# Cross-attention and FFN in one core: the prologue in another order, the first weights over two queues, one scores stage ahead of the second FFN layer

## The chip, the core and the metric

The kernel runs on one core of one Trainium2 chip. Its engines are TensorE (PE in the profile, PEld for its weight loads), VectorE (DVE), ScalarE (ACT) and GpSimd (POOL); SyncE (SP) issues most of the DMAs and ACT the rest. The metric is device time in microseconds (us), the median of the runs shown. Everything is float32 at the edges.

## What is computed

```python
x = x + attention(layernorm(x), ctx)      # 2 x 1024 x 256, context 2 x 77 x 192, 8 heads of 64
x = x + 0.5 * ffn(layernorm2(x))          # inside ffn: residual = its input, h = LN(x) * gamma + beta
# attention: q = x Wq, k = ctx Wk, v = ctx Wv, softmax(q k^T / 8) v, then Wo, + bo
# ffn(x) = x + 0.5 * (silu(h w1 + b1) w2 + b2), w = (q - 128) * scale, scale shared by 128 rows
# w1 is 256 x 1024, w2 is 1024 x 256, both stored as int32 with float scales
```

The second line stands for `x + _ffn_ref(_layernorm(x))`: the FFN's input is a layer norm of x, and the FFN norms it once more.

## The kernel before, in words

**Tiles.** The 2048 rows of x are 16 tiles of 128 rows, handled as eight pairs; pair a has the tiles 2a and 2a+1 (`a` runs from 0 to LAST = 7), pairs 0 to 3 belong to batch 0 and 4 to 7 to batch 1. Nothing is held in a lower precision: each operand of the large products is split in a rounded part (`_hi`) and the rest (`_lo`), both of type float32r, and three products (hi hi, hi lo, lo hi) are summed.

**Prologue, once.** The context is transposed (`ctxT`), keys and values are projected (`project`, L735), Wq is transposed and centred (`transpose_wq`). Then Wq and K of a batch are multiplied to one matrix M (`make_m(b, c)`, L766; halves c = 0, 1, in four parts M b.0 to M b.3), and V and Wo to VW (`make_vw(b, n)`, L779; five blocks in three parts VW b.0 to VW b.2). So the scores of a pair are its transposed rows times M, and its attention output is the transposed probabilities times VW. The int32 weights w1 become float in four pieces, each by ACT (`shift_w1`, then `split_w1`) and POOL (`dequantize_w1`, `lower_w1`), w2 in two halves by DVE (`dequantize_w2`, `lower_w2`) and ACT (L490 to L493).

**A pair.** `x_transposes` (XT), `scores` (S, two tiles of 24 products), softmax on DVE, ACT and POOL (`shift_scores`, `exponential`, `invert_sums`, `normalize`), `prob_transposes` (PT, 5 products), `attention_out` (AO, 15 products), `add_attention` on DVE, the root of the variance on POOL (`rsqrt2`), `make_hn` on DVE, `h_transposes` (HT), `scale_h` on ACT, `split_h` on DVE, `fc1` (four parts of 12 products), `hidden` on ACT (Silu, then the rounded part), `lower_y` on POOL, `fc2` (two tiles of 24 products), `finish_tile` on DVE, and the store.

**What sets the order.** Every engine's program is a list written by hand: TensorE's from L856 on, DVE's from L638, ACT's from L445, POOL's from L323, the DMA queue of SP from L223 and that of ACT from L353. An engine works through its list in that order and waits on semaphores. The accumulators are six names, S0, S1, H0, H1, T0 and T1; the table `order` (L62) says which result goes to which of them and in which turn, and a product waits until the last holder of its accumulator has been read (`emptied`, `wait_freed`). In the steady state a round of TensorE is: scores of pair a, the second FFN layer of pair a-2's second tile, `h_transposes(a-1)`, the first FFN layer of pair a-1 with the transposes of the probabilities of pair a between its parts, attention output of pair a, `x_transposes(a+1)`, and the second FFN layer of pair a-1's first tile.

**Warm-up.** Before the context is there TensorE multiplies zeros (`warm(8)`, L857), and once more while ctxT is copied (L865). A float32 product is two records of PE in the trace, a float32r product one.

**Waits that matter below.** `fc1(0, 0)` stands behind a wait for all four pieces of w1 (L905). `prob_transposes(a, j)` waits for `normalize(a, j)` on POOL. `h_transposes(a)` waits for both tiles of `make_hn(a)`, which wait for POOL's `rsqrt2(a)`. `fc2(0, 0)` waits for the lower parts of w2 (L848), which DVE makes, and for `lower_y`. ACT's `residual(a)` is needed by `add_b2(a)` on POOL, and that by `finish_tile`.

Of the kernel before, what the change touches and what calls it, by code (L numbers as in the profile page):

```python
# [25 lines left out]
def build_program(nc, x, ctx_in, wq, wk, wv, wo, bo, gamma, beta, q1, s1, b1, q2, s2, b2, out):  # L26
# [53 lines left out]
    with ExitStack() as stack:  # L80
# [138 lines left out]
        with nc.Block() as block:  # L219

            @block.sync
            def _(sp):
# [35 lines left out]
            def _(pool):  # L258
# [23 lines left out]
                def rsqrt2(a):  # L282

                    o = a % 2
                    for j in range(UT):
                        pool.wait_ge(mv2_done, a * UT + j + 1)
                        nc.gpsimd.tensor_scalar(vars2[:, o, 1, j:j + 1], mv2[:, o, j, 1:2], 1.0 + EPS, EPS * EPS,
                                                ALU.mult, ALU.add).then_inc(vars2_done, 1)
                        pool.wait_ge(vars2_done, a * 3 + j + 1)
                        nc.gpsimd.tensor_tensor(rstd2[:, o, 1, j:j + 1], vars2[:, o, 1, j:j + 1], neg_half[:, 0:1],  # L290
                                                ALU.pow).then_inc(rstd2_done, 1)
# [686 lines left out]
```

## Time and profile before

| | us |
|---|---|
| median of 3 runs | 189.31 (188.37 to 191.15) |
| the profiled execution | 188.6 |
| its span in the trace | 186.8 |
| PE busy | 180.7 (97%) |
| DVE, ACT, POOL busy | 122.4, 122.5, 116.2 |

The span is the time from the first to the last instruction of the trace; the profiled execution lasted 1.8 us longer than its span. TensorE is busy 97% of the span, but this busy time counts a record from its start to its modelled end, and the records overlap: one lasts about 0.28 us and the next starts 0.11 us after it. So the places where TensorE does nothing are read from the starts of neighbouring records and from the waits, not from the share. The eight rounds look alike from about 58.6 us on; what comes before is the prologue with the pairs 0 and 1.

### The profile page before, as it was taken

The numbers are of one execution on the slowest core, as the hardware profiler recorded it, in microseconds if no ns is written. First come the engines' busy times: TensorE is split into PE (matmuls) and PEld (weight loads), VectorE is DVE, ScalarE is ACT, GpSimd is POOL, SyncE is SP. The second block draws the span as 40 slices with busy tenths as digits, with TensorE's granted clock in tenths as the row PEclk, the third lists the DMA queues.
The fourth block names the chain that finished last, engine by engine and source line by source line (L and its number), as shares of the span: only waits on it lengthen the run. The fifth ranks groups of instructions, "written<-read, shape, count | busy, mean of one in ns | idle before, by whom it ended". The sixth has DMA issues, their size and how long they took to land.

```text
span 186.8 us, 3886 instructions
## 1 busy us (share of the span) xinstructions
PE 180.7 (97%) x1502; PEld 177.0 (95%) x1502; DVE 122.4 (66%) x261; ACT 122.5 (66%) x230; POOL 116.2 (62%) x159
## 2 busy tenths in 40 slices
PE   7999899899899999999999999999999999999994
PEld 7999699689899999999999999999999999999994
DVE  0287988899969464964496557937594768255341
ACT  3287880599918981898368944896289817962580
POOL 5032998569983977099707972597439762776220
PEclk9999999999999999999999999999999999999999
DMA  6997990000000100010001000100001000100101
GB/s 171 325 399 185 357 353 13 2 0 4 2 0 0 60 0 0 4 56 0 4 0 56 4 0 0 33 30 0 0 4 56 0 4 0 56 4 0 56 4 56
DMA packets 9480, 10.72 MB, mean 57 GB/s; under 512 B 2268, under 2 KB 8183, under 8 KB 9335
## 3 DMA queue, kind: packets, MB, share of 16 engines
q1 hardware_dynamic: 8837, 9.70, 15.7%
q10 hardware_dynamic: 626, 0.79, 1.5%
q8 instruction: 12, 0.20, 0.4%
q14 instruction: 5, 0.04, 0.1%
HBM read 8.38 MB, written 2.10 MB: 56 GB/s over the span
## 4 chain that ended last, share of the span: by engine, by line
PE 78%; DVE 9%; POOL 9%; ACT 1%; issue 1%
PE T L852 22%; PE H L838 21%; PE T L823 11%; PE S L802 11%; PE S L809 4%; PE S L755 3%; POOL q_sb L316 3%; POOL w_lo L321 3%; PE S L733 2%; DVE w_lo L631 2%; POOL probs L279 1%; DVE q_sb L625 1%; PE T L740 1%; PE H L740 1%; POOL rstd L290 1%
## 5 line engine op out<-in xcount | busy, mean ns | idle before, releaser
L311 POOL TENSOR_TENSOR y_lo<-y,y_hi 128x512 fp32r<-128x512 f32 x28 | 37.6, 1363 | 2.1 <-ACT y_hi L434 1.6
L279 POOL TENSOR_TENSOR probs<-probs,rsum 128x616 f32<-128x616 f32 x16 | 19.1, 1218 | 31.4 <-DVE rsum L583 31.4
L852 PE MATMUL T<-w_hi,y_hi 128*128 128x256 f32 x128 | 36.7, 286 | 0.6 <-DVE x_sb L594 0.6
L838 PE MATMUL H<-hT_hi,w_hi 128*128 128x256 f32 x128 | 36.7, 287 | 0.1
L838 PE MATMUL H<-hT_lo,w_hi 128*128 128x256 f32 x128 | 35.5, 277 | 0.0
L838 PE MATMUL H<-hT_hi,w_lo 128*128 128x256 f32 x128 | 35.5, 277 | 0.0
L852 PE MATMUL T<-w_lo,y_hi 128*128 128x256 f32 x128 | 35.5, 277 | 0.0
L852 PE MATMUL T<-w_hi,y_lo 128*128 128x256 f32 x128 | 35.4, 277 | 0.0
L430 ACT ACTIVATE y<-H,vec 128x256 f32<-128x256 f32 x64 | 26.5, 467 | 6.6 <-PE H L838 6.6
L403 ACT ACTIVATE probs<-probs,rstd 128x616 f32<-128x616 f32 x16 | 12.9, 807 | 27.1 <-DVE probs L571 27.1
L588 DVE TENSOR_TENSOR pT_lo<-S,pT_hi 128x640 fp32r<-128x640 f32 x16 | 13.1, 823 | 18.1 <-ACT pT_hi L407 18.1
L852 PEld LDWEIGHTS T<-w_hi,y_hi 128*128 128x128 f32 x128 | 24.1, 188 | 0.9 <-DVE x_sb L594 0.9
L838 PEld LDWEIGHTS H<-hT_hi,w_hi 128*128 128x128 f32 x128 | 24.1, 188 | 0.5 <-issue 0.5
L852 PEld LDWEIGHTS T<-w_lo,y_hi 128*128 128x128 f32 x128 | 24.1, 189 | 0.0
L838 PEld LDWEIGHTS H<-hT_lo,w_hi 128*128 128x128 f32 x128 | 24.1, 188 | 0.0
L852 PEld LDWEIGHTS T<-w_hi,y_lo 128*128 128x128 f32 x128 | 24.1, 188 | 0.0
L838 PEld LDWEIGHTS H<-hT_hi,w_lo 128*128 128x128 f32 x128 | 24.1, 188 | 0.0
L823 PE MATMUL T<-vw_hi,pT_hi 128*128 128x256 f32 x80 | 22.4, 280 | 0.0
L823 PE MATMUL T<-vw_lo,pT_hi 128*128 128x256 f32 x80 | 22.1, 277 | 0.0
L823 PE MATMUL T<-vw_hi,pT_lo 128*128 128x256 f32 x80 | 22.1, 277 | 0.0
L434 ACT ACTIVATE y_hi<-y 128x512 fp32r<-128x512 f32 x32 | 20.2, 632 | 1.0
L564 DVE TENSOR_REDUCE smax<-S 128x8 f32<-128x616 f32 x16 | 12.8, 799 | 12.0 <-PE S L802 11.5
(127 smaller groups left out, 460.6 us busy)
## 6 DMA issues: line engine op xcount, KB each, us to landing
q_sb<-in_L_ffn_fc_q SPq DMA_DIRECT2D x2, 1024.0 KB, 8.0
out_x<-x_sb SPq DMA_DIRECT2D x16, 128.0 KB, 1.8
x_sb<-in_x SPq DMA_DIRECT2D x7, 256.0 KB, 8.2
s_sb<-in_L_ffn_fc_scales SPq DMA_DIRECT2D x2, 512.0 KB, 12.0
s_sb<-in_L_ffn_fc_scales SPq DMA_DIRECT2D x1, 1024.0 KB, 7.7
wq_sb<-in_L_xattn_Wq SPq DMA_DIRECT2D x1, 512.0 KB, 5.6
wo_sb<-in_L_xattn_Wo SPq DMA_DIRECT2D x1, 512.0 KB, 8.1
wk_sb<-in_L_xattn_Wk ACTq DMA_DIRECT2D x1, 384.0 KB, 4.1
```

The lines of the kernel that those rows point to most:

```text
L279: nc.gpsimd.tensor_tensor(p, p, rsum[:, j, :].unsqueeze(2).to_broadcast([P, HEADS, J]), ALU.mult).then_inc(norm_done, 1)
L311: nc.gpsimd.tensor_tensor(y_lo[:, two, :], y[:, two, :], f32(y_hi[:, two, :]), ALU.subtract).then_inc(y_lo_done, 1)
L403: nc.scalar.activation(probs[:, j, 0:HJ], probs[:, j, 0:HJ], ACT.Exp, scale=rstd1[:, t:t + 1]).then_inc(exp_done, 1)
L430: ins = nc.scalar.activation(y[:, m, :], r[:, q * W:(q + 1) * W], ACT.Silu, bias=b1_sb[:, m:m + 1])
L434: nc.scalar.activation(y_hi[:, two, :], y[:, two, :], ACT.Copy).then_inc(y_hi_done, 1)
L564: nc.vector.tensor_reduce(smax[:, j, :].rearrange("p (n h) -> p n h", n=2), s, AX_X, ALU.max).then_inc(max_done, 1)
L588: nc.vector.tensor_tensor(flat(pT_lo[:, j, :, :]), ps[bank][:, 0:JC * P], flat(f32(pT_hi[:, j, :, :])), ALU.subtract).then_inc(freed[bank], 1)
L802: ins = mm(o, xt[:, c, j * P:(j + 1) * P], m[:, b, c, h, 0:HALF], start=n == 0, stop=n == len(steps) - 1)
L809: ins = nc.tensor.transpose(r[:, m * P:(m + 1) * P], probs[:, j, m * P:(m + 1) * P], ident[:, :])
L823: ins = mm(r[:, 0:D], p[:, j, m, :], v[:, b * JC + m, :], start=n == 0, stop=n == len(steps) - 1)
L838: ins = mm(r[:, q * W:(q + 1) * W], wt[:, c, m * P:(m + 1) * P], ht[:, c, :], start=c == q == i == 0, stop=c == q == 1 and i == 2)
L852: ins = mm(o, yt[:, m, j * P:(j + 1) * P], wt[:, m, :], start=m == 0 and i == 0, stop=m == M - 1 and i == 2)
```

## The change

The program does the same products, copies and transfers; only three of the warm-up products go, and wk comes by two DMAs where it was one. What moves:

- **Loads.** The first half of wk stays the first DMA of ACT's queue; its second half is the second of SP's, ahead of wq. `warm(8)` is `warm(5)`. `project("K", ...)` waits for both halves.
- **M and VW of batch 1.** `make_m(1, 1)` moves from between the transposes of the probabilities of pair 0 to behind `make_vw(1, 2)`, just ahead of `fc1(0, 0)`, and its two parts share accumulator S0. `make_vw(1, 0)` is cut in two, and its pieces stand around `prob_transposes(0, 0)`.
- **w1.** Its four pieces are now cut so that pieces 0 and 1 are the left columns of both row halves. POOL dequantizes two, normalizes pair 0, lowers two, dequantizes two, makes the roots of pair 0 (`root2`), and only then lowers the last two; `residual_roots` is what was left of `rsqrt2`. `fc1(0, 0)` waits for two pieces, `fc1(0, 2)` for four.
- **Pair 1.** `fc1(0, 2)` stands between the two transposes of probabilities, as in all later pairs. `x_transposes(2)` goes ahead of `attention_out(1, *)`, and `fc2(0, 0)` goes behind `scores(2, *)`, so that the scores of pair 2 (the third) are made first.
- **The other engines** follow: DVE does `stats1(1)` early, takes `lower_w2(1)` behind `add_attention(1, *)`; POOL cuts `lower_y(0, *)` in pieces between the roots of pair 1; ACT does `x_hi(2)` before `hidden(0, 2)` and `residual(0)` behind `exponential(2, 0)`.

In TensorE's list, around the transposes of the probabilities of pair 0 (L809; L786 is VW, L774 is M, L755 a transpose of x or hn), it stood so before:

```order
L755 MATMUL S<-ident,x_sb 128x128 x4
...
L774 MATMUL T<-kT,wqT 128x77
L809 MATMUL S<-ident,probs 128x128 x5
L774 MATMUL H<-kT,wqT 128x77
...
L809 MATMUL S<-ident,probs 128x128 x5
L786 MATMUL H<-wo_sb,vT 128x256 x3
L823 MATMUL T<-vw_hi,pT_hi 128x256
```

And so it stands there now (L838 are the transposes, L814 is VW, L852 the attention output):

```order
L800 MATMUL T<-kT,wqT 128x77
L814 MATMUL H<-wo_sb,vT 128x256
L838 MATMUL S<-ident,probs 128x128 x5
L814 MATMUL H<-wo_sb,vT 128x256 x2
L838 MATMUL S<-ident,probs 128x128 x5
L852 MATMUL T<-vw_hi,pT_hi 128x256
```

One of the three products of VW1.0 now fills the place before the first transposes, two stand between them, and M1's second half is gone from there.

In POOL's list, from the first dequantization of w1 to the first normalization of pair 1, before (L316 dequantizes w1, L279 normalizes, L321 lowers w1, L287 and L290 are the root of the second norm, L272 and L274 that of the first):

```order
L316 TENSOR_TENSOR q_sb<-q_sb,s_sb 128x512 x3
L279 TENSOR_TENSOR probs<-probs,rsum 128x616 x2
L316 TENSOR_TENSOR q_sb<-q_sb,s_sb 128x512
L321 TENSOR_TENSOR w_lo<-q_sb,w_hi 128x512 x4
L272 TENSOR_SCALAR veps<-mv 128x2
L274 TENSOR_TENSOR rstd<-veps,neg_half 128x2
L287 TENSOR_SCALAR vars<-mv 128x1
L290 TENSOR_TENSOR rstd<-vars,neg_half 128x1
```

Now (L319 dequantizes, L280 normalizes, L324 lowers w1, L273 and L275 are the first norm's root):

```order
L319 TENSOR_TENSOR q_sb<-q_sb,s_sb 128x512 x2
L280 TENSOR_TENSOR probs<-probs,rsum 128x616 x2
L324 TENSOR_TENSOR w_lo<-q_sb,w_hi 128x512 x2
L319 TENSOR_TENSOR q_sb<-q_sb,s_sb 128x512 x2
L287 TENSOR_SCALAR vars<-mv 128x1
L290 TENSOR_TENSOR rstd<-vars,neg_half 128x1
L287 TENSOR_SCALAR vars<-mv 128x1
L290 TENSOR_TENSOR rstd<-vars,neg_half 128x1
L273 TENSOR_SCALAR veps<-mv 128x2
L275 TENSOR_TENSOR rstd<-veps,neg_half 128x2
L324 TENSOR_TENSOR w_lo<-q_sb,w_hi 128x512 x2
```

Two of the four lowered pieces of w1 stand behind the roots now, and the roots of the second norm stand ahead of that of the first.

In DVE's list, from the dequantization of w2 to the first maximum of pair 2, now (L650 dequantizes w2, L613 is the lower part of the transposed probabilities, L578 that of VW, L584 that of the transposed x, L656 that of w2, L619 to L623 add the attention output and take its statistics, L629 is hn, L589 the maximum):

```order
L650 SCALAR_TENSOR_TENSOR q_sb<-q_sb,s_sb 128x1024 x2
L613 TENSOR_TENSOR pT_lo<-S,pT_hi 128x640
L578 TENSOR_TENSOR vw_lo<-T,vw_hi 128x512
...
L613 TENSOR_TENSOR pT_lo<-S,pT_hi 128x640
L578 TENSOR_TENSOR vw_lo<-T,vw_hi 128x256
L584 TENSOR_TENSOR xT_lo<-S,xT_hi 128x512
L656 TENSOR_TENSOR w_lo<-q_sb,w_hi 128x1024
L619 TENSOR_TENSOR x_sb<-T,x_sb 128x256
...
L656 TENSOR_TENSOR w_lo<-q_sb,w_hi 128x1024
L629 SCALAR_TENSOR_TENSOR hn<-x_sb,mv,rstd 128x256 x2
L589 TENSOR_REDUCE smax<-S 128x8
```

Before, both halves of w2 were lowered one behind the other ahead of the additions, and the lower part of x stood behind them.

The diff, without the parts that only rename a column or pass an index on:

```diff
              ("M0.0", "H1"), ("M0.1", "T0"), ("M0.23", "S0"), ("VW0.2", "T1"), ("VW0.0", "H0"), ("S0.0", "S0"), ("S0.1", "S1"),
-             ("VW0.1", "T1"), ("XT1", "S1"), ("M1.0", "H1"), ("M1.1", "T0"), ("PT0.0", "S0"), ("M1.2", "H0"), ("M1.3", "T1"), ("PT0.1", "S1"),
-             ("VW1.0", "H1"), ("AO0.0", "T0"), ("AO0.1", "T1"), ("S1.0", "S0"), ("S1.1", "S1"), ("HT0", "H0"), ("VW1.1", "T0"), ("VW1.2", "T1")]
+             ("VW0.1", "T1"), ("XT1", "S1"), ("M1.0", "H1"), ("M1.1", "T0"), ("VW1.0", "H0"), ("PT0.0", "S0"), ("PT0.1", "S1"),
+             ("AO0.0", "T1"), ("AO0.1", "T0"), ("S1.0", "S0"), ("S1.1", "S1"), ("HT0", "H0"), ("VW1.1", "T0"), ("VW1.2", "T1"), ("M1.23", "S0")]
     for a in range(1, NA):
         if a > 1:
-            order += [(f"S{a}.0", "S0"), (f"S{a}.1", "S1"), (f"F2.{a - 2}.1", "T1"), (f"HT{a - 1}", "S0")]
+            order += [(f"S{a}.0", "S0"), (f"S{a}.1", "S1")] + [("F2.0.0", "T0")] * (a == 2) + [(f"F2.{a - 2}.1", "T1"), (f"HT{a - 1}", "S0")]
         order += [(f"F1.{a - 1}.{p}", f"H{1 - p % 2}") for p in range(HP)]
         order += [(f"PT{a}.0", "S1"), (f"PT{a}.1", "S0"), (f"AO{a}.0", "T0"), (f"AO{a}.1", "T1")]
-        order += [(f"XT{a + 1}", "S1")] * (a < LAST) + [(f"F2.{a - 1}.0", "T0")]
+        order += [(f"XT{a + 1}", "S1")] * (a < LAST) + [(f"F2.{a - 1}.0", "T0")] * (a > 1)
...
                 sp.dma_start(ctx_sb[:, :, :], ctx_v).then_inc(ctx_in_sem, 16)
+                sp.dma_start(wk_sb[:, 1, :], wk[CC:DC, :]).then_inc(wk_in, 16)
                 sp.dma_start(wq_sb[:, :, :], wq.rearrange("(n p) f -> p n f", p=P)).then_inc(wq_in, 16)
...
+                def root2(a, j):
                     o = a % 2
...
+                def residual_roots(a):
+                    o = a % 2
                     nc.gpsimd.tensor_scalar(vars2[:, o, 0, :], mv2[:, o, :, 1], EPS, None, ALU.add).then_inc(vars2_done, 1)
...
-                    c, cols = n // 2, slice(n % 2 * F // 2, (n % 2 + 1) * F // 2)
+                    c, cols = n % 2, slice(n // 2 * F // 2, (n // 2 + 1) * F // 2)
...
                 pool.wait_ge(s1_in, 16 * C)
-                for n in range(2 * C - 1):
-                    dequantize_w1(n)
+                dequantize_w1(0)
+                dequantize_w1(1)
                 normalize(0, 0)
                 normalize(0, 1)
-                dequantize_w1(2 * C - 1)
-                for n in range(2 * C):
-                    lower_w1(n)
+                lower_w1(0)
+                lower_w1(1)
+                dequantize_w1(2)
+                dequantize_w1(3)
+                root2(0, 0)
+                root2(0, 1)
                 rsqrt1(1)
-                rsqrt2(0)
+                lower_w1(2)
+                lower_w1(3)
+                residual_roots(0)
                 pool.wait_ge(b2_done, 1)
-                for a in range(1, NA):
+                normalize(1, 0)
+                normalize(1, 1)
+                lower_y(0, 0)
+                lower_y(0, 1)
+                rsqrt1(2)
+                lower_y(0, 2)
+                root2(1, 0)
+                root2(1, 1)
+                lower_y(0, 3)
+                residual_roots(1)
+                add_b2(0)
+                for a in range(2, NA):
                     normalize(a, 0)
                     normalize(a, 1)
                     if a < LAST:
                         rsqrt1(a + 1)
                     for p in range(HP):
                         lower_y(a - 1, p)
-                    rsqrt2(a)
+                    root2(a, 0)
+                    root2(a, 1)
+                    residual_roots(a)
...
-                act.dma_start(wk_sb[:, :, :], wk.rearrange("(n p) f -> p n f", p=CC)).then_inc(wk_in, 16)
+                act.dma_start(wk_sb[:, 0, :], wk[0:CC, :]).then_inc(wk_in, 16)
...
                 m_hi_part(1, 0)
                 m_hi_part(1, 1)
                 split_w1(1)
+                prob_hi(0, 0)
+                prob_hi(0, 1)
+                vw_hi_part(1, 0)
                 split_w1(2)
-                prob_hi(0, 0)
-                m_hi_part(1, 2)
-                m_hi_part(1, 3)
-                prob_hi(0, 1)
                 split_w1(3)
-                vw_hi_part(1, 0)
                 act.wait_ge(vec_in, 16 * 2)
                 scale_h(0)
                 exponential(1, 0)
-                vw_hi_part(1, 1)
                 exponential(1, 1)
-                vw_hi_part(1, 2)
-                nc.scalar.activation(table_probe[:, :], neg_half[:, 0:1], ACT.Silu)
+                nc.scalar.activation(table_probe[:, 1:2], neg_half[:, 0:1], ACT.Silu)
+                m_hi_part(1, 2)
+                m_hi_part(1, 3)
                 hidden(0, 0)
                 hidden(0, 1)
                 prob_hi(1, 0)
+                vw_hi_part(1, 1)
                 prob_hi(1, 1)
-                for n in range(2):
-                    half = slice(n * M // 2, (n + 1) * M // 2)
-                    act.wait_ge(w2_done, n + 1)
-                    nc.scalar.activation(w2_hi[:, half, :], w2_sb[:, half, :], ACT.Copy).then_inc(w2_hi_done, 1)
+                vw_hi_part(1, 2)
+                x_hi(2)
+                w2_hi_part(0)
                 hidden(0, 2)
+                w2_hi_part(1)
                 hidden(0, 3)
-                nc.scalar.activation(table_probe[:, :], neg_half[:, 0:1], ACT.Exp)
-                x_hi(2)
-                residual(0)
+                nc.scalar.activation(table_probe[:, 0:1], neg_half[:, 0:1], ACT.Exp)
                 for a in range(2, NA):
                     exponential(a, 0)
+                    if a == 2:
+                        residual(0)
                     scale_h(a - 1)
...
                 vw_lo_part(0, 2)
+                stats1(1)
                 vw_lo_part(0, 0)
                 shift_scores(0, 0)
                 shift_scores(0, 1)
...
                 invert_sums(0, 1)
                 vw_lo_part(0, 1)
                 x_lo(1)
+                prob_lo(0, 0)
                 m_lo_part(1, 0)
                 m_lo_part(1, 1)
-                prob_lo(0, 0)
-                m_lo_part(1, 2)
-                m_lo_part(1, 3)
                 prob_lo(0, 1)
                 vw_lo_part(1, 0)
-                stats1(1)
                 add_attention(0, 0)
                 add_attention(0, 1)
+                make_hn(0, range(1))
                 score_maxima(1, 0)
-                make_hn(0)
+                make_hn(0, range(1, UT))
                 subtract_maxima(1, 0)
                 shift_scores(1, 1)
                 split_h(0)
                 invert_sums(1, 0)
                 invert_sums(1, 1)
-                vw_lo_part(1, 1)
-                vw_lo_part(1, 2)
-                stats1(2)
+                m_lo_part(1, 2)
+                m_lo_part(1, 3)
                 dve.wait_ge(q2_in, 16)
                 dve.wait_ge(s2_in, 16)
                 dequantize_w2(0)
                 dequantize_w2(1)
                 prob_lo(1, 0)
+                vw_lo_part(1, 1)
+                stats1(2)
                 prob_lo(1, 1)
+                vw_lo_part(1, 2)
+                x_lo(2)
                 lower_w2(0)
-                lower_w2(1)
                 add_attention(1, 0)
                 add_attention(1, 1)
-                x_lo(2)
+                lower_w2(1)
                 make_hn(1)
                 for a in range(2, NA):
...
                         pe.wait_ge(h_half_split, f + 1)
+                    if f == 0 and p % 2 == 0:
+
+                        pe.wait_ge(w1_split, p + C)
                     r = emptied(name)
...
-                warm(8)
+                warm(5)
...
-                pe.wait_ge(wk_in, 16)
+                pe.wait_ge(wk_in, 16 * 2)
...
                 make_m(1, 0)
+                make_vw(1, 0, range(1))
                 pe.wait_ge(probs_ready, 1)
                 prob_transposes(0, 0)
-                make_m(1, 1)
+                make_vw(1, 0, range(1, 2))
                 prob_transposes(0, 1)
-                make_vw(1, 0)
                 attention_out(0, 0)
                 attention_out(0, 1)
                 scores(1, 0)
...
                 h_transposes(0)
                 make_vw(1, 1)
                 make_vw(1, 2)
-                pe.wait_ge(w1_split, 2 * C)
+                make_m(1, 1)
                 fc1(0, 0)
                 fc1(0, 1)
                 prob_transposes(1, 0)
+                fc1(0, 2)
                 prob_transposes(1, 1)
-                fc1(0, 2)
                 fc1(0, 3)
+                x_transposes(2)
                 attention_out(1, 0)
                 attention_out(1, 1)
-                x_transposes(2)
-                fc2(0, 0)
                 for a in range(2, LAST):
                     scores(a, 0)
                     scores(a, 1)
+                    if a == 2:
+                        fc2(0, 0)
                     fc2(a - 2, 1, range(1))
                     h_transposes(a - 1)
                     fc2(a - 2, 1, range(1, M))
```

## Rows read from the trace of the kernel before

**Rows 1.** Busy us of each engine by stretch: PE, PEld, DVE, ACT, POOL, PEclk, DMA share, GB/s.
```profile
37.00:49.00 12.00, 10.97 (x92) 10.42 (x91) 11.83 (x18) 11.83 (x21) 10.01 (x7) 1.00 0.01 2
```

**Rows 2.** Timeline of PE, start: start us, us, what, idle before and its releaser.
```profile
1.03 3.78 PE L733 MATMUL S<-warm_sb 128*128 128x128 f32 x16 [1.03 <-DVE warm_sb L638]
4.61 0.47 PE L863 MATMUL T<-ident,ctx_sb 77*96 77x77 f32 x2
...
5.80 1.29 PE L740 MATMUL T<-ctxT,wk_sb 96*128 96x154 f32 x8
...
7.98 0.60 PE L748 MATMUL H<-ident,wq_sb 128*128 128x128 f32 x4
...
12.44 1.06 PE L774 MATMUL S<-kT,wqT 64*128 64x77 f32 x16
```

**Rows 3.** DMAs of the page: queue, KB each, us from issue to landing.
```profile
wq_sb<-in_L_xattn_Wq SPq DMA_DIRECT2D x1, 512.0 KB, 5.6
...
wk_sb<-in_L_xattn_Wk ACTq DMA_DIRECT2D x1, 384.0 KB, 4.1
```

**Rows 4.** Timeline of SP: the issue of its first DMA.
```profile
0.72 0.41 SPq L223 DMA_DIRECT2D ctx_sb<-in_ctx  x1
```

**Rows 5.** Timeline of PE, the places of the prologue where it waits.
```profile
22.79 0.74 PE L809 MATMUL S<-ident,probs 128*128 128x128 f32 x5 [0.51 <-issue]
...
33.05 0.30 PE L802 MATMUL S<-m_hi,xT_lo 128*128 128x308 f32 x1
33.89 0.66 PE L755 MATMUL H<-ident,hn 128*128 128x128 f32 x4 [0.53 <-DVE hn L604]
34.38 2.33 PE L786 MATMUL T<-wo_sb,vT 128*128 128x256 f32 x10
36.84 0.36 PE L838 MATMUL H<-hT_hi,w_hi 128*128 128x256 f32 x1
...
40.94 0.77 PE L809 MATMUL S<-ident,probs 128*128 128x128 f32 x5 [0.41 <-POOL probs L279]
```

**Rows 6.** The same timeline, at the second FFN layer of pair 0.
```profile
49.02 0.38 PE L852 MATMUL T<-w_hi,y_hi 128*128 128x256 f32 x1 [0.65 <-DVE x_sb L594]
```

**Rows 7.** Timeline of POOL.
```profile
21.48 2.39 POOL L279 TENSOR_TENSOR probs<-probs,rsum 128x616 f32<-128x616 f32 x2
...
25.06 5.04 POOL L321 TENSOR_TENSOR w_lo<-q_sb,w_hi 128x512 fp32r<-128x512 f32 x4
...
44.02 7.01 POOL L311 TENSOR_TENSOR y_lo<-y,y_hi 128x512 fp32r<-128x512 f32 x4
```

**Rows 8.** Timeline of DVE.
```profile
27.85 0.42 DVE L525 BATCH_NORM_STATS2 bn<-x_sb 128x6 f32<-128x256 f32 x1
...
28.93 0.39 DVE L594 TENSOR_TENSOR x_sb<-T,x_sb 128x256 f32<-128x256 f32 x1
...
37.32 0.79 DVE L580 TENSOR_REDUCE ssum<-probs 128x8 f32<-128x616 f32 x1
...
44.86 3.78 DVE L631 TENSOR_TENSOR w_lo<-q_sb,w_hi 128x1024 fp32r<-128x1024 f32 x2
...
51.97 0.48 DVE L604 SCALAR_TENSOR_TENSOR hn<-x_sb,mv,rstd 128x256 f32<-128x256 f32 x1 [0.76 <-POOL rstd L290]
53.17 0.48 DVE L604 SCALAR_TENSOR_TENSOR hn<-x_sb,mv,rstd 128x256 f32<-128x256 f32 x1 [0.72 <-POOL rstd L290]
53.77 0.80 DVE L564 TENSOR_REDUCE smax<-S 128x8 f32<-128x616 f32 x1
```

**Rows 9.** Timeline of ACT: the residual of pair 0.
```profile
49.94 1.08 ACT L420 ACTIVATE x_sb<-x_sb,res_shift,res_scale 128x256 f32<-128x256 f32 x2
```

**Rows 10.** The chain that ended last, in order of time: start us, us, what.
```profile
58.59 2.72 PE H L838 x24
...
78.30 2.73 PE H L838 x24
```

**Rows 11.** The page's costliest groups: xcount | busy us, mean ns | idle before, releaser.
```profile
L311 POOL TENSOR_TENSOR y_lo<-y,y_hi 128x512 fp32r<-128x512 f32 x28 | 37.6, 1363 | 2.1 <-ACT y_hi L434 1.6
```

More of the change, by code:

```diff
@@ L172, in m_home @@
         def m_home(b, n):
-            if b == 0 and n >= 2:
-                return "M0.23", (n - 2) * BANK
+            if n >= 2:
+                return f"M{b}.23", (n - 2) * BANK
             return f"M{b}.{n}", 0
@@ L280, in normalize @@
                                             ALU.mult).then_inc(norm_done, 1)
-                def rsqrt2(a):
+                def root2(a, j):
                     o = a % 2
[L285 to L291, printed above, removed]
+                    pool.wait_ge(mv2_done, a * UT + j + 1)
+                    nc.gpsimd.tensor_scalar(vars2[:, o, 1, j:j + 1], mv2[:, o, j, 1:2], 1.0 + EPS, EPS * EPS,
+                                            ALU.mult, ALU.add).then_inc(vars2_done, 1)
+                    pool.wait_ge(vars2_done, a * 3 + j + 1)
+                    nc.gpsimd.tensor_tensor(rstd2[:, o, 1, j:j + 1], vars2[:, o, 1, j:j + 1], neg_half[:, 0:1],
+                                            ALU.pow).then_inc(rstd2_done, 1)
+                def residual_roots(a):
+                    o = a % 2
                     nc.gpsimd.tensor_scalar(vars2[:, o, 0, :], mv2[:, o, :, 1], EPS, None, ALU.add).then_inc(vars2_done, 1)
@@ L434, in hidden, with w2_hi_part @@
                     nc.scalar.activation(y_hi[:, two, :], y[:, two, :], ACT.Copy).then_inc(y_hi_done, 1)
+                def w2_hi_part(n):
+                    half = slice(n * M // 2, (n + 1) * M // 2)
+                    act.wait_ge(w2_done, n + 1)
+                    nc.scalar.activation(w2_hi[:, half, :], w2_sb[:, half, :], ACT.Copy).then_inc(w2_hi_done, 1)
                 def shift_w1(n):
[L437 removed]
+                    c, cols = n % 2, slice(n // 2 * F // 2, (n // 2 + 1) * F // 2)
                     nc.scalar.activation(w1_sb[:, c, cols], q1_sb[:, c, cols], ACT.Copy, bias=-ZERO_POINT).then_inc(w1_shifted, 1)
                 def split_w1(n):
[L441 removed]
+                    c, cols = n % 2, slice(n // 2 * F // 2, (n // 2 + 1) * F // 2)
                     act.wait_ge(w1_done, n + 1)
@@ L510, in _ @@
                     if a < LAST:
-                        nc.scalar.activation(table_probe[:, :], neg_half[:, 0:1], ACT.Exp)
+                        nc.scalar.activation(table_probe[:, 0:1], neg_half[:, 0:1], ACT.Exp)
                         x_hi(a + 1)
@@ L598, in add_attention, with make_hn @@
                     nc.vector.bn_aggr(mv2[:, o, j, :], bn2[:, o, j, :]).then_inc(mv2_done, 1)
-                def make_hn(a):
-                    for j in range(UT):
+                def make_hn(a, js=range(UT)):
+                    for j in js:
                         t, o = a * UT + j, a % 2
@@ L777, in make_m, with make_vw @@
                             fill(homes[e][0], ins[e])
-                def make_vw(b, n):
-                    r = emptied(f"VW{b}.{n}")
-                    for q in range(min(2, JC - 2 * n)):
+                def make_vw(b, n, qs=range(2)):
+                    if qs[0] == 0:
+                        emptied(f"VW{b}.{n}")
+                    r = ps[place[f"VW{b}.{n}"][0]]
+                    for q in qs[:JC - 2 * n]:
                         m = 2 * n + q
```

15 lines of the change are left out of this document (7 added, 8 removed).

## The prediction

> **What bounds the kernel.** PE is busy in 180.7 of 186.8 us, so I looked first for where it is not. In the chain that ended last the steady rounds are PE records one behind another, 19.71 us from one first FFN layer (58.59) to the next (78.30) [rows 10]; the change leaves the rounds from pair 3 on as they are, so nothing is to be had there. In the prologue it is otherwise: the stretch from 37 to 49 us has DVE and ACT busy in 11.83 of 12 us each and PE in 10.97 [rows 1]. So the time that the change can move is the time that PE waits before the first FFN layer of pair 1, at 58.59 [rows 10]; whatever that start gains, all later rounds gain, if their own covers hold.
>
> PE's timeline shows the places. An idle time in brackets begins at a modelled end: a record of 0.30 us at 33.05 is followed, when nothing is missing, after 0.14 us, so a wait costs its idle time and some 0.16 us more. By that rule: before the transposes of the probabilities of pair 0, 0.51 + 0.16 = 0.67; before `h_transposes(0)`, 0.69; before the second transposes of pair 1, 0.57; before `fc2(0, 0)`, 0.81 [rows 5, 6]. And ahead of `fc1(0, 0)`: ten records of VW from 34.38, at (2.33 - 0.38)/10, some 0.2 us, would let it start at 36.4; it starts at 36.84, so 0.4, of which 0.1 is usual at such a change: 0.3 [rows 5]. These five are 3.04 us. At the start, 16 warm-up records go before ctxT, to 4.61 [rows 2].
>
> **The start.** Three warm-ups less are 6 of 16 records, of 0.236 us each: the warm-up ends at about 3.2 instead of 4.6 [rows 2]. ctxT then waits for the context, whose landing no row shows. wk, issued in the same moment and three times as large, landed at 0.7 + 4.1 = 4.8 [rows 3, 4]; the context must have landed by 4.4, when ctxT's weights are loaded, and can't be taken as earlier than the end of the warm-up. Bounds of the gain: 0 and 1.4. Nearest is wk's landing, and the context stands in the same traffic, so I take 0.3. wk in halves over both queues costs and brings nothing: K starts at 5.80, a full us behind wk's landing at 4.8, and starts at 5.5 now. wq gets 192 KB ahead of it on its queue; issued at about 1.2, behind the context, it landed 5.6 later, at 6.8, and is needed at 7.98, now 7.7 [rows 2 to 4]. wk's 384 KB in 4.1 us give 94 KB a us for one queue at worst; by that the half would cost 2.0, less the half that ACT's queue no longer carries: between 0 and 2.0, and I take 0.3, which the 0.9 of room hide. At its high end it would cost 1.1 us; the range has room for that.
>
> **Pair 0.** (a) One of three products of VW1.0 (2 records of 0.2) goes before the first transposes. They wait for POOL's normalization, which starts when DVE has the sums; the dequantization that stood ahead of it ends just as it starts [rows 7] and was no cause. So 0.37 of the 0.67 is filled: **-0.4**. (b) The second half of M1, 16 records or 1.0 us by those of batch 0 [rows 2], leaves the stretch before the attention output; there it hid ACT's and DVE's work on the transposed probabilities; a pass of DVE over such a tile is 0.8 us [rows 8], and I take 0.7 for ACT's. These were behind the split of w1, now ahead of m_lo on DVE. I find pT_lo(0, 0) at about 24.8 and PE ready at 24.5: a new wait, **+0.3**. (c) `h_transposes(0)` waits for hn, that for POOL's roots, and these stood behind four lowered pieces of w1 (5.04 us) and `rsqrt1(1)` [rows 7]. `stats1(1)`, 1.08 us (27.85 to 28.93 [rows 8]), no longer delays the addition, and POOL has two pieces (2.5 us) less ahead. I laid the durations of before in the new order. POOL: normalizations 21.2 to 23.6, four pieces of 1.26 to 28.6, roots at 29.5 and 30.9; DVE: hn at 31.6. PE: from 24.9 thirty records of attention in 3.5 us and 24 of scores in 3.4, to 31.8. The wait goes: **-0.65**, with 0.2 us of margin; if POOL is late by more, part of it comes back.
>
> **Pair 1.** (d) `fc1(0, 0)` has M1's second half, 1.0 us, ahead of it, so split_h (DVE: hn at 31.6, three passes of 0.8, then 0.7: 34.7) is done when PE arrives at 35.4: **-0.3**. That is 1.4 us earlier than before. (e) The 1.36 us of `fc1(0, 2)` (half of 2.72 [rows 10]) between the transposes cover one normalization (1.2 us, half of 2.39): **-0.57**. The first now wants POOL by 38.3; POOL lowers two pieces and makes the residual's roots to 36.5, normalizes to 37.7 and 38.9. (f) `fc2(0, 0)` waited for w2_lo and y_lo, not, as the row has it, for the addition, which reads another tile: w2_lo ended at 48.6 [rows 8]. Now the scores of pair 2, 3.4 us, stand in between: **-0.8**. They need `x_lo(2)`, at 45.0 by my list, and PE comes to them at 46.2.
>
> Together: -0.3 - 0.4 + 0.3 - 0.65 - 0.3 - 0.57 - 0.8 = -2.7.
>
> **What is late next.** Before, DVE came to the first maximum of pair 2 at 53.77, 16.45 us after `invert_sums(1, 0)` at 37.32, and 1.48 of this it waited for POOL's roots [rows 8]. The same list now starts at 35.35, has two parts of m_lo (0.86) more and a wait of 0.3 for pT_hi: 35.35 + 16.45 - 1.48 + 0.86 + 0.3 = 51.5. From there two passes of 0.8 to the first subtraction's end, then on ACT the exponential (taken as one such pass, 0.8), the residual (1.08 [rows 9]), which the change puts ahead of `scale_h(1)`, and half of scale_h (half of such a 1.08), on DVE the split of one half (0.7, from two passes of 256 columns like hn's 0.48, overlapped): 56.2 us, while PE could start `fc1(1, 0)` at 58.59 - 2.7 = 55.9. With wake-ups between the engines that is a stall of 0.4 us. Its bounds: none, and 1.3, if everything on DVE takes as long as it did and POOL's last roots are late again. One thing speaks for less: beside w2_lo (3.78 us for two halves) POOL's y_lo took 7.01 for four, 1.75 each, where the mean of all is 1.36 [rows 7, 8, 11]. So the two held each other up, and now only parts of them meet. The Trainium skill ("SBUF — State Buffer", section "SBUF: two separate sides") says that such operations take the shared port in turn, each for its whole length; by it the stall would be none where they don't meet, and the sum -2.7. I take **+0.3**: the sum is **-2.4**.
>
> The profiled execution, 188.6, becomes 186.2. It lies 0.7 below the median of 189.31; a median of few runs may fall on either, so I put the forecast at 186.6, 0.4 above.
>
> **Rivals.**
>
> 1. *The cover is too thin.* The end of the prologue turns from PE to the chain DVE, ACT, DVE of (f): DVE is busy in nearly all of 37 to 49, and the change takes nothing from it. For it: that share, and `residual(0)` in front of scale_h. Against: 1.48 us of waits for POOL go. Stall 1.3, and 0.4 at (c): gain 2.7 - 1.7 = 1.0, 187.6.
> 2. *The clock rises later.* The 16 warm-up records take 0.236 us each with 128 columns; K's with 154 columns 0.14 (16 in the 2.18 us from 5.80 to 7.98) [rows 2]: half speed, 1.2 GHz, until about 5.3, then 2.4. The granted clock's column prints 1.00, in a stretch past the rise as over the whole [rows 1]; for the start the records decide. Before the rise PE worked on without a break from 1.03; now it stands from 3.2 to 4.3. If the rise is late, each us of full-speed work costs another: K alone 2.2, half of K 1.1. Then the gain is 0.2 to 1.3: 187.3 to 188.4. For it: that break is the one new thing ahead of the rise. Against: it is short, and work resumes before the old rise. The Trainium skill ("TensorE: Matmul & The Clock Gate", section "Part 1: The HAM clock gate") has the array start throttled, with sustained activity releasing it; whether a break of this length counts, no row of this kernel shows.
> 3. *Slower: the same clock, longer.* If half speed lasts past K and the transposes of wq (0.9 us), the price is over 2.4, and the kernel is slower than before. Through V's projections, which have K's count of records (2.2), and twelve transposes (1.3), it is 5.7 us of work: 188.6 - 2.4 + 5.7 = 191.9. It decides from 2.4 us of work at half speed on, that is if K and a quarter of the rest of this stretch run so.
> 4. *More than the sum.* The context is there by 3.4 and the stall is none: -2.7 - 0.7, and no new wait in (b), -0.3: 3.7 less, 184.9.
> 5. *Nothing of it.* The waits that go are the ends of chains through DVE (sums, additions), and they come back one step later, at (b), (c) and `fc1(1, 0)`; the time is 188.3 to 188.9. Against: three of the waits, (d), (e) and (f), get work of more than their length put in front.
>
> **Chances and range.** Forecast (185.4 to 187.4) 0.55, rival 1 0.15, rival 2 0.12, rival 3 0.04, rival 4 0.09, rival 5 0.05. The range takes in the forecast, rival 1, rival 2 to its middle and a part of rival 4: 185.0 to 188.6. Two per cent, about what a measurement of this kernel can tell from no change, are 3.8 us: 185.5 against the median. Below it lie rival 4 and the low end of the forecast: 0.18. Slower by over 2% wants 193.1, the far end of rival 3: 0.03. The rest, 0.79, is within.
>
> **What would show it.** ctxT at about 4.3, K at 5.5 and records of 0.14 us in it (a later rise shows as 0.26). The first transposes of probabilities still idle, for some 0.3; a wait for pT_lo ahead of the attention output of pair 0. hn(0) ahead of the end of the scores of pair 1 and no idle before `h_transposes(0)`. `fc1(0, 0)` at 35.4, not 36.84. Transposes of pair 1 without an idle. `fc2(0, 0)` behind the scores of pair 2, with w2_lo's second half done in its first half. `fc1(1, 0)` at 56.2: if it stands later, behind DVE's hT_lo, rival 1 has it. From pair 3 on every round as long as before, 19.7 us; if one is longer, the forecast fails in a way that I have not priced.

## The result, and the profile after

| | us |
|---|---|
| changed kernel, median of 4 | 192.06 (191.8 to 192.63) |
| kernel before, median of 4 | 189.11 (188.37 to 191.15) |
| ratio, 95% interval | 1.0148 (1.0096 to 1.02) |
| profiled execution, span | 191.8, 190.0 (before 188.6, 186.8) |

The kernel became slower by 1.5%; I had forecast 186.6. The span grew by 3.2 us. The timeline of PE at the start of the changed kernel, to be held against [rows 2]:

```profile
1.04 2.50 PE L759 MATMUL S<-warm_sb 128*128 128x128 f32 x10 [1.04 <-DVE warm_sb L663]
4.70 0.47 PE L895 MATMUL T<-ident,ctx_sb 77*96 77x77 f32 x2 [1.16 <-DMA ctx_sb<-in_ctx]
4.96 0.46 PE L895 MATMUL H<-ident,ctx_sb 77*96 77x77 f32 x2
5.21 0.72 PE L759 MATMUL S<-warm_sb 128*128 128x128 f32 x2
5.89 2.39 PE L766 MATMUL T<-ctxT,wk_sb 96*128 96x154 f32 x8
8.08 2.26 PE L766 MATMUL H<-ctxT,wk_sb 96*128 96x154 f32 x8
10.13 0.66 PE L774 MATMUL H<-ident,wq_sb 128*128 128x128 f32 x4
```

```profile
PE T L895 <- DMA ctx_sb<-in_ctx: 1.2, 1, 1.2
PE S L759 <- DVE warm_sb L663: 1.0, 1, 1.0
PE S L781 <- DVE pT_lo L613: 1.0, 1, 1.0
PE H L870 <- DVE hT_lo L638: 0.7, 1, 0.7
PE S L781 <- DVE probs L596: 0.3, 1, 0.3
PE T L852 <- DVE pT_lo L613: 0.2, 1, 0.2
```

The waits of before are gone, and others stand in their place: 1.0 before the transposes of x of pair 2 (L781), 0.3 before `h_transposes(1)`, 0.7 before the first FFN layer of pair 1 (L870). Behind them are DVE and POOL, here in their two timelines:

```profile
40.92 4.30 DVE L650 SCALAR_TENSOR_TENSOR q_sb<-q_sb,s_sb 128x1024 f32<-128x1024 int32 x2
...
52.32 1.19 DVE L656 TENSOR_TENSOR w_lo<-q_sb,w_hi 128x1024 fp32r<-128x1024 f32 x1
...
54.36 1.51 DVE L629 SCALAR_TENSOR_TENSOR hn<-x_sb,mv,rstd 128x256 f32<-128x256 f32 x1 [0.45 <-POOL rstd L290]
...
59.72 1.03 DVE L636 CAST hT_hi<-hT 128x256 fp32r<-128x256 f32 x1 [0.78 <-ACT hT L433]
```

```profile
41.88 4.48 POOL L314 TENSOR_TENSOR y_lo<-y,y_hi 128x512 fp32r<-128x512 f32 x2
...
54.30 1.29 POOL L314 TENSOR_TENSOR y_lo<-y,y_hi 128x512 fp32r<-128x512 f32 x1
...
59.31 1.29 POOL L308 TENSOR_TENSOR x_sb<-x_sb,b_half 128x512 f32<-128x512 f32 x1 [1.81 <-ACT x_sb L441]
```

w2's two dequantizations took 4.30 us beside two y_lo that took 4.48, not 2.5. hn (0.48 in [rows 8]) took 1.51 beside y_lo, the cast of h 1.03 beside b2's addition; it takes 0.28 in the kernel before and in the best version below. The lowered halves of w2 are quicker than before (1.2 each; 3.78 for two in [rows 8]), since nothing stands beside them now. So the hold-up moved from there to three places that PE waits behind. The first FFN layer of pair 1 starts at 61.27 instead of 58.4: 2.8 us of the 3.2.

### The profile page after: what moved, and what is told of

It is laid out like the page before. It is cut to its first block, busy times and chain, and to the rows that moved or that the text cites. A ratio compares the mean times of both kernels' runs of the same rounds, so it can differ in the third digit from the quotient of the medians.

```text
span 190.0 us, 3876 instructions
## 1 busy us (share of the span) xinstructions
PE 182.6 (96%) x1496; PEld 178.1 (94%) x1496; DVE 125.0 (66%) x261; ACT 122.9 (65%) x230; POOL 115.9 (61%) x159
## 4 chain that ended last, share of the span: by engine, by line
PE 79%; DVE 11%; ACT 3%; POOL 3%; DMA 2%; issue 1%
PE H L870 20%; PE T L884 19%; PE T L852 13%; PE S L831 12%; PE S L781 4%; PE S L838 4%; DVE q_sb L650 2%; DMA ctx_sb<-in_ctx 2%; PE T L766 2%; PE H L766 2%; DVE hn L629 1%; PE T L814 1%; DVE probs L596 1%; DVE smax L589 1%; DVE hT_hi L636 1%
## 5 line engine op out<-in xcount | busy, mean ns | idle before, releaser
L314 POOL TENSOR_TENSOR y_lo<-y,y_hi 128x512 fp32r<-128x512 f32 x28 | 38.1, 1382 | 3.2 <-ACT y_hi L455 2.9
L870 PE MATMUL H<-hT_hi,w_hi 128*128 128x256 f32 x128 | 36.9, 289 | 0.7 <-DVE hT_lo L638 0.7
L280 POOL TENSOR_TENSOR probs<-probs,rsum 128x616 f32<-128x616 f32 x16 | 19.2, 1218 | 29.9 <-DVE rsum L608 29.9
L870 PE MATMUL H<-hT_lo,w_hi 128*128 128x256 f32 x128 | 35.5, 277 | 0.0
L870 PE MATMUL H<-hT_hi,w_lo 128*128 128x256 f32 x128 | 35.5, 277 | 0.0
L613 DVE TENSOR_TENSOR pT_lo<-S,pT_hi 128x640 fp32r<-128x640 f32 x16 | 13.1, 821 | 18.1 <-ACT pT_hi L428 18.1
L870 PEld LDWEIGHTS H<-hT_hi,w_hi 128*128 128x128 f32 x128 | 24.1, 189 | 1.0 <-DVE hT_lo L638 0.9
L870 PEld LDWEIGHTS H<-hT_lo,w_hi 128*128 128x128 f32 x128 | 24.1, 188 | 0.0
L870 PEld LDWEIGHTS H<-hT_hi,w_lo 128*128 128x128 f32 x128 | 24.0, 188 | 0.0
L852 PE MATMUL T<-vw_hi,pT_hi 128*128 128x256 f32 x80 | 22.4, 280 | 0.4 <-DVE pT_lo L613 0.2
L852 PE MATMUL T<-vw_lo,pT_hi 128*128 128x256 f32 x80 | 22.1, 277 | 0.0
L852 PE MATMUL T<-vw_hi,pT_lo 128*128 128x256 f32 x80 | 22.1, 277 | 0.0
L589 DVE TENSOR_REDUCE smax<-S 128x8 f32<-128x616 f32 x16 | 12.7, 796 | 11.2 <-PE S L831 10.8
```

The costliest lines, as they stand in the source:

```text
L280: nc.gpsimd.tensor_tensor(p, p, rsum[:, j, :].unsqueeze(2).to_broadcast([P, HEADS, J]), ALU.mult).then_inc(norm_done, 1)
L314: nc.gpsimd.tensor_tensor(y_lo[:, two, :], y[:, two, :], f32(y_hi[:, two, :]), ALU.subtract).then_inc(y_lo_done, 1)
L589: nc.vector.tensor_reduce(smax[:, j, :].rearrange("p (n h) -> p n h", n=2), s, AX_X, ALU.max).then_inc(max_done, 1)
L613: nc.vector.tensor_tensor(flat(pT_lo[:, j, :, :]), ps[bank][:, 0:JC * P], flat(f32(pT_hi[:, j, :, :])), ALU.subtract).then_inc(freed[bank], 1)
L852: ins = mm(r[:, 0:D], p[:, j, m, :], v[:, b * JC + m, :], start=n == 0, stop=n == len(steps) - 1)
L870: ins = mm(r[:, q * W:(q + 1) * W], wt[:, c, m * P:(m + 1) * P], ht[:, c, :], start=c == q == i == 0, stop=c == q == 1 and i == 2)
```

## The experiments

Each ratio is to the kernel before as it ran beside it: its median was 188.9 beside runs 1 to 4, 189.0 beside 5 to 8, 188.9 beside 9 to 11 and 189.8 beside 12.

**1. Eight warm-ups in the changed kernel.** `warm(5)` -> `warm(8)`.

> The changed kernel with eight warm-up products again, all else as changed. Theory (the clock's rise comes late because PE stands still after five warm-ups until the context is there): K's sixteen records take some 2.2 us instead of 4.2, the transposes of wq start at about 8.0 instead of 10.1, and the whole is about 2.1 us shorter than the changed kernel, near 189.9. Rival (the rise is late for another reason, such as the execution's own offset, and the warm-ups don't decide it): K's records stay at 0.26 us and the time at 192. Second rival (the rest of the change is a gain that the clock hid): 187.

190.68, ratio 1.0114 (1.0069 to 1.0159). K takes 2.22 us (5.70 to 7.92): the clock is back. But the time fell by 1.4, not 2.1. The new wait in its list:

```profile
PE T L766 <- DMA wv_sb<-in_L_xattn_Wv: 1.1, 1, 1.1
```

V starts at 10.52, where it started at 9.29 in the kernel before; half speed had hidden this wait.

**2. Five warm-ups in the kernel before.** `warm(8)` -> `warm(5)`.

> The kernel before with five warm-up products instead of eight, all else as before. Theory (the break after five warm-ups delays the clock's rise): K's records at 0.26 us, wq's transposes at about 10, and the time about 2.1 us above the kernel before, near 191.2. Rival (the new load order or the reordered lists of the change are what delays it): no difference to the kernel before, 189.1.

191.23, ratio 1.0135 (1.0092 to 1.0177): +2.3 from this line alone. Here the context came earlier and K took 4.27 us (5.42 to 9.69) all the same:

```profile
3.92 0.46 PE L863 MATMUL T<-ident,ctx_sb 77*96 77x77 f32 x2 [0.38 <-DMA ctx_sb<-in_ctx]
...
5.42 2.42 PE L740 MATMUL T<-ctxT,wk_sb 96*128 96x154 f32 x8 [0.27 <-DMA wk_sb<-in_L_xattn_Wk]
7.64 2.26 PE L740 MATMUL H<-ctxT,wk_sb 96*128 96x154 f32 x8
9.69 1.06 PE L748 MATMUL H<-ident,wq_sb 128*128 128x128 f32 x4
```

There is a second idle, 0.27 for wk. And half speed didn't end with K: the twelve records of the transposes took 2.56 us (9.69 to 12.25) where they took 1.31 (7.98 to 9.29). V starts 2.96 later than before, and the span of this execution, 189.8, is 3.0 longer; it is the slowest of the four.

**3. and 4. GpSimd's root first, then the residual first.**

```diff
-                lower_y(0, 0)
-                lower_y(0, 1)
                 rsqrt1(2)
+                lower_y(0, 0)
+                lower_y(0, 1)
```

> As the run with eight warm-ups, and on GpSimd the root of the first norm of pair 2 goes ahead of the first two y_lo of pair 0, so that these don't stand beside DVE's dequantization of w2. Theory (DVE and GpSimd hold each other up there: 4.30 us for the dequantization where it was 2.35): it falls back to about 2.4 us, the transposes of x of pair 2 no longer wait 1.2 us for pT_lo, and the time falls by 0.8 to 1.9 us against the run with eight warm-ups, near 188.5. Rival (what DVE gains there it loses at the next wait, for y_lo, for w2_hi or for the roots of pair 1): within 0.4 us.

A miss: 191.55, 0.9 more than run 1. The dequantizations fell to 3.21 us and the transposes of x came 1.15 earlier (43.97, not 45.12), but `rsqrt1(2)` waited 4.71 us for DVE's statistics and held GpSimd up. Its y_lo then stood beside the lowered halves of w2, which took 1.90 and 1.58 instead of 1.2, and PE waited in `fc2(0, 0)`:

```profile
PE T L884 <- POOL y_lo L314: 1.6, 1, 1.6
```

The rival was right here: the gain was lost at y_lo.

> As the run before it, and ACT adds the residual of pair 0 ahead of the exponential of pair 2 instead of behind it. Theory (ACT idles there for 3.9 us, and the residual's 1.08 us, with GpSimd's addition of b2 that follows it, stand between the scores of pair 2 and scale_h of pair 1, and so hold the first FFN layer of pair 1): the wait of 0.85 us before that layer goes, another 0.6 to 1.2 us less. Rival (that layer waits for DVE's softmax passes, whatever ACT does): within 0.3 us.

191.06. The first FFN layer of pair 1 followed `h_transposes(1)` by 2.87 us instead of 3.73, the wait of 0.7 gone, as expected; but the medians differ by 0.5 only, within their scatter (190.32 to 192.12).

**5. The old loads, eight warm-ups, the new order.** wk whole on ACT's queue.

> The changed kernel with eight warm-ups and with wk whole on ACT's queue as before: what is left is the new order alone. Theory (the half of wk on SP's queue lets x and b2 on ACT's pass it and pushes wv, which landed at 10.5 instead of 8.5 and held V's projections by 1.2 us): V starts at about 9.3 instead of 10.5, and the time is 1.2 us below the changed kernel with eight warm-ups, near 189.4, so the new order alone is no gain. Rival (wv is late since the whole traffic is slower in that run): V stays at 10.5 and the time at 190.7.

189.65, ratio 1.0055 (1.0023 to 1.0087). V at 9.23. The order alone is a small loss: its `fc1(0, 0)` is at 35.76, 1.1 ahead of before (36.84), its `fc1(1, 0)` at 58.89, 0.5 behind.

**6. wk in two halves in the kernel before.**

```diff
+sp.dma_start(wk_sb[:, 1, :], wk[CC:DC, :])      # second on SP's queue
-act.dma_start(wk_sb[:, :, :], ...)
+act.dma_start(wk_sb[:, 0, :], wk[0:CC, :])
```

> The kernel before with wk in two halves over both queues, all else as before, eight warm-ups among it. Theory (the split alone delays wv): wv lands at about 10.4, V's projections start at 10.5 instead of 9.3, the time is some 1.2 us above the kernel before, near 190.1. Rival (the split is harmless and K gains by it): 188.9 or less.

189.84, ratio 1.0057 (1.0033 to 1.008): +0.9, a little less than expected. The DMAs of this run, KB each and us to landing, against [rows 3]:

```profile
wv_sb<-in_L_xattn_Wv SPq DMA_DIRECT2D x1, 384.0 KB, 8.6
x_sb<-in_x ACTq DMA_DIRECT2D x1, 256.0 KB, 4.6
wk_sb<-in_L_xattn_Wk ACTq DMA_DIRECT2D x1, 192.0 KB, 3.3
wk_sb<-in_L_xattn_Wk SPq DMA_DIRECT2D x1, 192.0 KB, 4.0
```

wk is whole at 1.2 + 4.0 = 5.2 us, where it was at 4.8; x of pair 0, not yet needed, comes 2 us sooner (6.5 us from issue before), and wv, next on the path, nearly 2 later (6.8 before). PE waits 1.5 us for it. Over the executions with K at full speed and eight warm-ups, V started at 10.20 to 10.70 with wk split (runs 1, 3, 4 and 6) and at 9.23 to 9.73 with wk whole (before, runs 5, 7 and 8).

**7. The residual ahead of the exponential** (in 5.)

```diff
+                    if a == 2:
+                        residual(0)
                     exponential(a, 0)
-                    if a == 2:
-                        residual(0)
```

> As the run with the old loads and eight warm-ups, and the residual of pair 0 goes ahead of the exponential of pair 2 on ACT. Theory (residual and b2's addition stand in the way of scale_h and of DVE's cast): the first FFN layer of pair 1 starts 0.9 to 1.2 us earlier, the time is near 188.4. Rival (the earlier addition on GpSimd meets other work of DVE and gives it back): within 0.3 us of that run.

188.52, 1.1 below run 5; ratio to before 0.9993 (0.9964 to 1.0022). The first FFN layer of pair 1 follows `h_transposes(1)` by 2.86 us instead of run 5's 3.72, and the cast of h takes 0.28 instead of 1.03. The edit takes the residual's 1.08 us out of the chain and b2's addition away from the cast at once; how much each was worth isn't told apart.

**8. DVE and GpSimd kept apart** (in 7.)

```diff
 dequantize_w2(0)
-dequantize_w2(1)
+stats1(2)
 prob_lo(1, 0)
 vw_lo_part(1, 1)
-stats1(2)
+dequantize_w2(1)
...
 x_lo(2)
-lower_w2(0)
 add_attention(1, 0)
+lower_w2(0)
...
 root2(1, 0)
-root2(1, 1)
 lower_y(0, 3)
+root2(1, 1)
...
-x_hi(2)
 w2_hi_part(0)
+x_hi(2)
```

> As the run before it, with DVE's and GpSimd's passes over SBUF kept apart: DVE dequantizes half of w2, takes the statistics of pair 2 and the first pT_lo, and only then the other half; one addition goes ahead of the first lowered half of w2; GpSimd lowers the last y between the two roots of pair 1; ACT rounds w2 ahead of x_hi(2). Theory (the gain that I forecast is there once the two engines don't hold each other up): the dequantizations take 1.2 us each, no wait of 1.2 us before the transposes of x of pair 2, the first FFN layer of pair 1 at 56 to 56.7, the time near 186.7. Rival (the work of DVE and GpSimd on the shared operands is the bound itself, and order only moves the waits): within 0.5 us of the run before it.

**187.36**, ratio 0.9922 (0.9891 to 0.9953): faster than both kernels, though by 1.6 and not by the 2.4 that I had forecast for the change. All that PE waits for in it:

```profile
PE S L758 <- DVE warm_sb L662: 1.0, 1, 1.0
PE T L851 <- DVE pT_lo L612: 0.2, 1, 0.2
PE T L851 <- DVE vw_lo L577: 0.2, 1, 0.2
PE S L780 <- DVE probs L595: 0.2, 1, 0.2
```

and four of DVE's passes:

```profile
38.70 2.07 DVE L649 SCALAR_TENSOR_TENSOR q_sb<-q_sb,s_sb 128x1024 f32<-128x1024 int32 x1
...
43.08 1.22 DVE L649 SCALAR_TENSOR_TENSOR q_sb<-q_sb,s_sb 128x1024 f32<-128x1024 int32 x1
...
49.00 2.10 DVE L655 TENSOR_TENSOR w_lo<-q_sb,w_hi 128x1024 fp32r<-128x1024 f32 x1
...
55.43 0.28 DVE L635 CAST hT_hi<-hT 128x256 fp32r<-128x256 f32 x1
```

The two engines still meet twice: the first dequantization (2.07) and the second lowered half of w2 (2.10, 1.19 in run 7) stand beside y_lo. The first FFN layer of pair 1 is at 56.98, 1.5 ahead of before, and PE reaches it without a wait.

**9. to 11. The break and the warm-ups.** Five warm-ups ahead of ctxT and four behind it, then eleven, both in the kernel before; then ten in run 8's kernel.

> The kernel before with five warm-ups ahead of ctxT and four behind it, where it has eight and one: the same nine in sum, but with the break until the context is there. Theory (the break itself delays the clock's rise): K's records at 0.26 us again and the time at 191 or more. Rival (what counts is how much of the dense warm-up work TensorE has done before K, wherever it stands): K starts at about 6.0, its records take 0.14 us, the time is some 0.3 us above the kernel before, 189.3.

191.43, ratio 1.0112 (1.0075 to 1.0149). The timeline of PE:

```profile
1.03 2.50 PE L733 MATMUL S<-warm_sb 128*128 128x128 f32 x10 [1.03 <-DVE warm_sb L638]
4.92 0.46 PE L863 MATMUL T<-ident,ctx_sb 77*96 77x77 f32 x2 [1.39 <-DMA ctx_sb<-in_ctx]
5.18 0.46 PE L863 MATMUL H<-ident,ctx_sb 77*96 77x77 f32 x2
5.44 2.00 PE L733 MATMUL S<-warm_sb 128*128 128x128 f32 x8
7.23 2.26 PE L740 MATMUL T<-ctxT,wk_sb 96*128 96x154 f32 x8
9.28 1.53 PE L740 MATMUL H<-ctxT,wk_sb 96*128 96x154 f32 x8
```

Nine warm-ups in sum, and still K begins at half speed and ends near full speed (2.05 us for its first eight, 1.4 for the rest): with the same nine and no break, in the kernel before, all of K ran at full speed. So in this pair the break counts, not how many stand before K.

> The kernel before with eleven warm-ups. They end at about 6.0 at half speed, or a little over 5.3 if the clock rises under them. Theory (eight are enough in most executions, and not in the few that take 191 us): the median moves up by 0.3 to 0.9 us with ctxT's start, and the slowest runs are no longer 2 us above the fastest. Rival (the slow executions have another cause): they stay, at 191.5 or more.

189.41 (188.76 to 190.15, 10 runs), before 188.90 (188.48 to 190.62, 14 runs): 0.5 more, and no run over 190.2. Its profiled execution:

```profile
1.04 5.06 PE L733 MATMUL S<-warm_sb 128*128 128x128 f32 x22 [1.04 <-DVE warm_sb L638]
...
6.41 0.72 PE L733 MATMUL S<-warm_sb 128*128 128x128 f32 x2
7.09 1.33 PE L740 MATMUL T<-ctxT,wk_sb 96*128 96x154 f32 x8
```

The clock rose only at about 7.1 here, behind 24 warm-up records and ctxT at half speed, and just ahead of K.

> The best version so far (old loads, DVE's and GpSimd's passes kept apart, the residual early) with ten warm-ups instead of eight. Theory (two more only put off ctxT, whose context is there): 0.2 to 0.6 us above its 187.4. Rival (the clock's rise is the weak point even with eight): the same or less, 187.0, with a narrower spread.

187.31, ratio 0.9915 (0.9893 to 0.9938): no difference to eight, as the rival had it. In its profiled execution the clock rose under the warm-ups (20 records in 3.92 us), and K started at 5.70, no later than with eight.

**12. The dequantization alone** (in 7.)

> As the run with the old loads, eight warm-ups and the early residual (188.5), with one thing of the best version alone: DVE dequantizes the second half of w2 behind the statistics of pair 2 and the first pT_lo instead of at once. Theory (the hold-up of 1.95 us at the dequantization, and with it the wait before the transposes of x of pair 2, is the larger part of the 1.2 us between that run and the best version): the two dequantizations fall from 4.3 to 3.3 us or less, the transposes of x start at 42.7 instead of 43.7 on the origin of the best version, the time is 187.5 to 187.9. Rival (the best version's gain comes from the additions and the roots further back): within 0.3 us of 188.5.

187.68 (187.39 to 189.61), ratio 0.987 (0.9793 to 0.9947), but to a kernel before that ran higher and wider beside it (188.69 to 191.11). The median is 0.8 below run 7's. The two dequantizations took 2.08 and 1.22 us, as expected, and PE no longer waits before the transposes of x. Its profiled execution was its slowest, 189.6, and shows the clock's late rise with eight warm-ups:

```profile
1.04 3.79 PE L758 MATMUL S<-warm_sb 128*128 128x128 f32 x16 [1.04 <-DVE warm_sb L662]
4.88 0.46 PE L894 MATMUL T<-ident,ctx_sb 77*96 77x77 f32 x2
5.14 0.46 PE L894 MATMUL H<-ident,ctx_sb 77*96 77x77 f32 x2
5.39 0.72 PE L758 MATMUL S<-warm_sb 128*128 128x128 f32 x2
6.08 2.39 PE L765 MATMUL T<-ctxT,wk_sb 96*128 96x154 f32 x8
8.26 2.26 PE L765 MATMUL H<-ctxT,wk_sb 96*128 96x154 f32 x8
```

## Why the prediction was wrong

**The start** failed, by 2.5 us. I took -0.3 for the earlier ctxT and nothing for the clock; ctxT was +0.1, since the context's DMA ended late (ctxT at 4.70, PE waiting). The clock, which I gave 0.12 as rival 2 with 1.1 to 2.2 us and 0.04 as rival 3, is the mechanism: 2.1 us, all of K at half speed and no more in the changed kernel's profiled execution. Runs 1, 2 and 9 show it from three sides; of the eight executions of runs 2 and 9 seven took 190.8 or more, where 19 of 21 of the kernel before, beside them, took 189.4 or less. I judged the break too short to count; in run 2 two short ones, 0.38 and 0.27 us, went with half speed through K and the transposes. The Trainium skill ("TensorE: Matmul & The Clock Gate", section "Part 1: The HAM clock gate") ties full speed to sustained activity; runs 2 and 9 agree, but the profiled execution of run 12, busy from 1.04 and at half speed until about 10.3, doesn't follow from it.

**wk over both queues**, which I took to cost nothing, failed too. I weighed wq, which has room, and not wv, which had 0.8: it landed at 8.5 and was needed at 9.3. Worth 0.9 (run 6), hidden in the changed kernel by the slow clock, and so not additive: 2.3 and 0.9 alone, together with the order 3.0.

**(a) to (d)** were right. `fc1(0, 0)` stands 28.01 us behind the transposes of wq instead of 28.86: -0.85, where the terms gave -1.05; in run 5 it is 27.84, so -1.0. The new wait for pT_lo in (b) is there, 0.2 to 0.4.

**(e) and (f)** were right in what they took away: no wait is left before the second transposes of pair 1 or in `fc2(0, 0)`.

**What is late next** was the other failing step, also by 2.5 us. I took +0.3 with a bound of 1.3. It is four waits: before the transposes of x of pair 2 (1.2 with the tail), in the attention output of pair 1 (0.3 to 0.4: its 30 records take 3.92 us, from 46.70 to 50.62, where they took 3.50), before `h_transposes(1)` (0.5) and before `fc1(1, 0)` (0.85), 2.8 in all. I had read the slow pairs of [rows 7, 8] as a price that would be saved, and kept DVE's duration of 2.35 for the dequantization, though the change put GpSimd's y_lo from behind POOL's roots beside it. DVE alone needs 2.4 for two, GpSimd 2.5; together they ran from 40.92 to 46.36. The Trainium skill ("SBUF — State Buffer", section "SBUF: two separate sides") has a DVE instruction with two inputs from SBUF and a GpSimd instruction that reads it block each other, one for the other's whole length; a dequantization of 2.1 to 2.3 instead of 1.2 beside y_lo fits this. The last of the four waits is gone in run 7, which takes the residual from ahead of scale_h and b2's addition from beside the cast of h; the residual's 1.08 was in my sum, the slower cast (1.03, not 0.28) was not. Rival 1 named the chain, but not this cause.

The whole: +0.1 + 2.1 - 0.85 - 0.57 - 0.8 + 2.8 = +2.8 at `fc1(1, 0)`, as measured. The two terms of (e) and (f) stand in it as forecast: the traces show the waits gone, not their worth. The rounds behind it add 0.4, mostly in the first of them, where the transposes of the probabilities come 0.2 late.

**Open.** Why the clock sometimes rises late with eight warm-ups (run 12's execution) isn't settled; in it PE had no idle between the first warm-up and K that the trace prints, though ctxT started 0.27 later than in the kernel before (4.88, 4.61). How long half speed lasts varies as well: to about 9.8 in run 9, 10.2 in the changed kernel and 12.25 in run 2. So what exactly puts the rise off stays open; that five warm-ups with a break do it nearly always, and eight without one seldom, is what the runs show. That before's few executions near 191 are of this kind is likely by their time, but none of them was profiled. With eleven, ten runs stayed below 190.2: in the one that was profiled K was covered, not the rise made earlier; ten are too few to be sure.

## What to carry to other kernels

When a placeholder that keeps an engine busy is shortened, price what it keeps up, not only what it delays. When a load is split over two queues, look for who is overtaken: the bytes ahead of each later transfer are the cost. When passes of DVE and GpSimd over SBUF are moved, lay both lists side by side in time: a duration from the old order holds only with the old neighbour.
